# Local attention on one core: the first head group's products with V move behind the next slot's projections, and the transposed probabilities get one PSUM bank

## The reference, cut to what matters

```
qkv = shift_tokens(x) @ Wqkv            # 128 -> 3 * 1024
q, k = l2norm(q) * qs, l2norm(k) * ks   # 16 heads of 64
q, k = rotary(q), rotary(k)
sim  = q @ k.T * 8, windows of 32 tokens, each sees itself and the one before
out  = softmax(sim) @ v @ Wo ; x1 = x + out
xn   = layernorm(shift_tokens(x1))
x2   = x1 + (xn @ W1a + b) * gelu(xn @ W1g + b) @ W2 + b2
```

## Time and profile before

| what | value |
|---|---|
| time, median of 3 runs | 2543.07 us (2542.53 to 2543.28) |
| profiled execution | 2539.95 us, span of its instructions 2538.1 us |
| PE busy | 2370.2 us, 93% of the span |
| DVE, ACT, POOL busy | 77%, 68%, 61% |
| mean granted TensorE clock | 0.985 of full speed |

### The profile page before, as it was taken

One profiled execution on the slowest core, in us unless ns is written; L12 is line 12 of the kernel. 1 busy time (PEld: TensorE's weight loads), 2 busy tenths in 40 slices (PEclk: granted clock), 3 DMA queues, 4 the chain that ended last, 5 costly groups with the idle time before them and its releaser, 6 DMA issues.

```text
span 2538.1 us, 63009 instructions
## 1 busy us (share of the span) xinstructions
PE 2370.2 (93%) x22929; PEld 1578.0 (62%) x22929; DVE 1958.3 (77%) x2967; ACT 1720.5 (68%) x3296; POOL 1552.6 (61%) x1359
## 2 busy tenths in 40 slices
PE   6888789997899999999999999999999999999995
PEld 3555456665466666666666666666666666666664
DVE  4899857776777777777778787777777787787774
ACT  5888545443577777777776776777777777767763
POOL 4777723232666667667666666666676676666662
PEclk8999989999999999999999999999999999999997
DMA  2312110000122122222221221221222222212211
GB/s 73 110 60 64 54 45 1 1 1 9 39 69 62 50 66 69 51 63 61 62 62 51 73 62 50 73 63 50 63 70 53 62 59 65 62 51 73 62 50 48
DMA packets 102906, 140.33 MB, mean 55 GB/s; under 512 B 63040, under 2 KB 63936, under 8 KB 102336
## 3 DMA queue, kind: packets, MB, share of 16 engines
q1 hardware_dynamic: 102848, 139.57, 20.6%
HBM read 56.39 MB, written 1.31 MB: 23 GB/s over the span
## 4 chain that ended last, share of the span: by engine, by line
PE 52%; DVE 16%; issue 5%; ACT 1%; DVEq 1%; DMA 0%; POOL 0%; SPq 0%; POOLq 0%; ACTq 0%
PE f_psA L1751 14%; PE f_psO L1735 9%; PE f_psA L1745 7%; PE f_psD L1755 5%; DVE f_mx L1535 5%; PE f_psS L1715 4%; DVE f_Pr L1542 4%; DVE f_den L1546 3%; PE f_psO L1818 3%; PE f_psS L1697 3%; PE f_psD L1845 3%; PE f_psP L1715 2%; DVE f_x L1592 1%; PE f_psS L1687 1%; DVE f_hT L1558 1%
## 5 line engine op out<-in xcount | busy, mean ns | idle before, releaser
L1751 PE MATMUL f_psA<-f_W,f_xT 128*128 (+1 forms) x1152 | 603.2, 617 | 8.6 <-DVE f_m L1569 5.5
L1344 POOL TENSOR_TENSOR f_Pr<-f_Pr,f_rden 128x384 f32<-128x384 f32 x384 | 310.6, 829 | 484.9 <-DVE f_rden L1548 484.9
L1569 DVE TENSOR_TENSOR f_m<-f_psA,f_tab 128x1024 f32<-128x1024 f32 x384 | 458.8, 1222 | 161.5 <-ACT f_sq L1439 159.0
L1369 POOL TENSOR_TENSOR f_qkr<-f_qkr,f_rn 128x1024 f32<-128x1024 f32 x192 | 360.7, 1897 | 0.1
L1439 ACT ACTIVATE f_sq<-f_psA 128x512 f32<-128x512 f32 x384 | 228.9, 596 | 166.1 <-PE f_psA L1751 161.2
L1361 POOL TENSOR_TENSOR f_qkr<-f_m 128x512 f32<-128x512 f32 x192 | 245.3, 1278 | 142.8 <-DVE f_m L1569 142.8
L1751 PEld LDWEIGHTS f_psA<-f_W,f_xT 128*128 128x128 f32 x1152 | 184.3, 190 | 147.5 <-DVE f_m L1569 70.5
L1735 PE MATMUL f_psO<-f_PT,f_V 96*64 96x64 f32 x6144 | 261.5, 228 | 4.3 <-ACT f_PT L1414 0.2
L1735 PEld LDWEIGHTS f_psO<-f_PT,f_V 96*64 96x64 f32 x6144 | 211.1, 138 | 69.1 <-issue 54.7
L1535 DVE TENSOR_REDUCE f_mx<-f_psS 128x8 f32<-128x768 f32 x192 | 178.8, 931 | 89.0 <-PE f_psS L1697 89.0
L1362 POOL TENSOR_TENSOR f_qkr<-f_m 128x512 f32<-128x512 f32 x192 | 243.3, 1267 | 0.0
(11 more groups left out here) (166 smaller groups left out, 4578.4 us busy)
## 6 DMA issues: line engine op xcount, KB each, us to landing
f_V<-f_Vt SPq DMA_DIRECT2D x96, 384.0 KB, 4.2
f_V<-f_Vt SPq DMA_DIRECT2D x96, 256.0 KB, 3.6
f_W<-in_f_W SPq DMA_DIRECT2D x48, 344.0 KB, 3.6
m_Cb<-m_BC_rows SPq DMA_DIRECT2D x64, 256.0 KB, 3.1
f_W<-in_f_W SPq DMA_DIRECT2D x48, 296.5 KB, 4.2
f_V<-f_Vt SPq DMA_DIRECT2D x48, 128.0 KB, 5.4
f_xsA<-xall SPq DMA_DIRECT2D x97, 32.0 KB
f_xsA<-xall SPq DMA_DIRECT2D x97, 31.8 KB
```

What stands on the lines that cost most here:

```text
L1344: pool.tensor_tensor(pv, pv, rv.unsqueeze(3).broadcast_to([P, 2, 2, KEYS]), ALU.mult).then_inc(Pr_ready[g][j], 1)
L1369: pool.tensor_tensor(qv, qv, rn[:, j * H:(j + 1) * H].unsqueeze(2).broadcast_to([P, H, DH]), ALU.mult).then_inc(qkr_ready[j], 1)
L1569: dve.tensor_tensor(m12[:, j, :, half].rearrange("p m (h d) -> p m h d", d=DH), psA[n % 2][:, :].rearrange("p (h d) -> p h d", d=DH).unsqu ...
L1751: pe.matmul(psA[n % 2][:, :], xT[:, t, :], weights(i, W_QKV + n * 512, 512), start=True, stop=True).then_inc(A_full[n_fill], 1)
```

## The change

Unit v's group 0 is now split. Only its first four heads are transposed at the end of the slot (`transpose_probs(0, 0, v)`). The other transposes and all of its products with V run in the next slot, between `project(1)` and the transposes of q and k, mixed with the remaining projections and the group-1 transposes. All four transposes of a unit use the one bank psP, so each waits for ACT's copy of the one before, and psS holds nothing but scores. The token transpose and `scores(1)` change places with `project(4)`; in the E slot the `w1(0, 0)` and `w1(0, 1)` come ahead of the projections; in the D slot the gate products of chunks 0 and 1 come later. On POOL, `rotate` of k stands between the last two `normalise_probs`, and `scale` of k opens the next slot. On DVE, `gated` moves ahead of `maximum(v, 0)`, and x2 comes ahead of hatC. The ACT order follows. The same matrix products and element-wise operations are done.

```diff
@@ GpSimd, slot @@
-                if "A" in stages:
-                    rotate(u, t, 1)
-                if "B" in stages:
-                    normalise_probs(v, 0, 0)
-                    normalise_probs(v, 0, 1)
+                if "B" in stages:
+                    scale(v, q, 1)
                 if "A" in stages:
                     scaled_tables(u + 1, i + t, 1 - t)
                     rotate(u, t, 0)
                 if "B" in stages:
-                    normalise_probs(v, 1, 0)
-                    normalise_probs(v, 1, 1)
-                if "A" in stages:
-                    scale(u, t, 0)
-                    scale(u, t, 1)
+                    normalise_probs(v, 0, 0)
...
+                if "B" in stages:
+                    normalise_probs(v, 0, 1)
+                if "A" in stages:
+                    scale(u, t, 0)
+                if "B" in stages:
+                    normalise_probs(v, 1, 0)
+                if "A" in stages:
+                    rotate(u, t, 1)
+                if "B" in stages:
+                    normalise_probs(v, 1, 1)
@@ VectorE, slot @@
+                if "E" in stages:
+                    dve.wait_ge(ge_ready, (i - 1) * 3)
+                    gated(2)
+                if "A" in stages:
                     table_products(2)
                     table_products(3)
...
+                if "E" in stages:
+                    dve.wait_ge(ge_ready, (i - 1) * 3)
+                    gated(0)
+                    gated(1)
                 if "B" in stages:
                     maximum(v, 0)
                     less_maximum(v, 0)
...
-                if "C" in stages:
-                    dve.wait_ge(rstdC_ready, wu + 1)
-
-                    at_least(dve, xn_full, i - 1)
-                    dve.tensor_scalar(hatC[:, t, :], xsC[:, t, :], momC[:, 0:1], rstdC[:, :], ALU.subtract, ALU.mult).then_inc(hatC_ready, 1)
                 if "E" in stages:
                     dve.wait_ge(w2_full, i - 1)
                     dve.wait_ge(x1b_ready, (i - 1) * 2)
                     alone(dve, passed)
                     dve.tensor_tensor(tiles_of(i - 2), psD[0][:, T2:2 * T2].rearrange("p (t d) -> p t d", d=D), tiles_of(i - 2), ALU.add).then_inc(x2_done, 2)
+                if "C" in stages:
+                    dve.wait_ge(rstdC_ready, wu + 1)
+
+                    at_least(dve, xn_full, i - 1)
+                    dve.tensor_scalar(hatC[:, t, :], xsC[:, t, :], momC[:, 0:1], rstdC[:, :], ALU.subtract, ALU.mult).then_inc(hatC_ready, 1)
@@ TensorE @@
-                def transpose_probs(g, j):
-                    unit = (v, wu)[g]
+                def transpose_probs(g, j, unit):
 
                     pe.wait_ge(Pr_ready[g][j], unit + 1)
-                    if g != j:
-
-                        pe.wait_ge(S_free[1], unit + 1)
+                    if j == 1:
+                        pe.wait_ge(P_free[g][0], unit + 1)
                     elif g == 1:
-                        pe.wait_ge(P_free[0][0], unit + 1)
-                    elif "C" in stages:
-                        pe.wait_ge(P_free[1][1], wu + 1)
-                    dst = probs_bank(g, j)
+                        pe.wait_ge(P_free[0][1], unit + 1)
+                    else:
+                        at_least(pe, P_free[1][1], unit)
...
                 if "B" in stages:
-                    transpose_probs(0, 0)
-                    transpose_probs(0, 1)
-                    times_v(0, 0)
-                    times_v(0, 1)
+                    transpose_probs(0, 0, v)
```

More of the change, by code:

```diff
@@ L1227, in at_least @@
                 eng.wait_ge(s, n)
-        def probs_bank(g, j):
-            return psP if g == j else psS[:, g, :].rearrange("p (n q) -> p n q", q=P)
         def bias_col(n):
@@ L1408, in slot, with evacuate_probs @@
                 u, v, wu = i * 2 + t, i * 2 + (t - 1), i * 2 + (t - 2)
-                def evacuate_probs(g, j):
-                    unit = (v, wu)[g]
+                def evacuate_probs(g, j, unit):
                     act.wait_ge(P_full[g][j], unit + 1)
-                    act.activation(PT[:, j, :, :], probs_bank(g, j)[0:KEYS, :, :], ACT.Copy).then_inc(P_free[g][j], 1)
+                    act.activation(PT[:, j, :, :], psP[0:KEYS, :, :], ACT.Copy).then_inc(P_free[g][j], 1)
                 def evacuate_v(j):
@@ L1454, in gate_gelu @@
                     act.activation(ge[0:FC[c], c, :], src[0:FC[c], :], ACT.Gelu, bias=bias_col(3 + c)[0:FC[c], :]).then_inc(ge_ready, 1)
+                if "A" in stages:
+                    square(0)
+                if "B" in stages and q == 1:
+                    act.activation(kT[:, 1, :, 0:WIN], kT[:, 0, :, P:P + WIN], ACT.Copy).then_inc(kprev_ready, 1)
+                if "A" in stages:
+                    square(1)
+                if "C" in stages:
+                    evacuate_probs(0, 1, wu)
                 if "D" in stages:
                     act.preload_act_table_set(GELU)
-                if "A" in stages:
-                    square(0)
-                if "D" in stages:
                     act.wait_ge(xn_full, i - 1)
@@ L1465, in slot @@
                 if "A" in stages:
-                    square(1)
-                if "B" in stages and q == 1:
-                    act.activation(kT[:, 1, :, 0:WIN], kT[:, 0, :, P:P + WIN], ACT.Copy).then_inc(kprev_ready, 1)
+                    square(2)
+                if "C" in stages:
+                    evacuate_probs(1, 0, wu)
+                if "A" in stages:
+                    square(3)
+                if "C" in stages:
+                    evacuate_out(0, wu, t)
                 if "D" in stages:
@@ L1602, in slot @@
                     dve.tensor_scalar(rn[:, H:2 * H], rn0[:, H:2 * H], 1e12, None, ALU.min).then_inc(rn_ready, 1)
-                if "E" in stages:
-                    dve.wait_ge(ge_ready, (i - 1) * 3)
-                    gated(0)
-                    gated(1)
                 if "C" in stages:
@@ L1757, in w1 @@
                         ins.then_inc(full[bank_of(c)[1]], 1)
+                if "E" in stages:
+                    pe.wait_ge(ge_ready, (i - 2) * 3 + 2)
+                    w1(0, 0, a_full)
+                    w1(0, 1, a_full)
                 if "A" in stages:
@@ L1762, in slot @@
                     project(0)
+                    project(1)
+                if "C" in stages:
+                    transpose_probs(0, 1, wu)
                 if "D" in stages:
@@ L1771, in slot @@
                     ins.then_inc(xn_full, 1)
-                if "A" in stages:
-                    project(1)
+                if "C" in stages:
+                    times_v(0, 0, wu, t)
                 if "E" in stages:
-                    pe.wait_ge(ge_ready, (i - 2) * 3 + 2)
-                    w1(0, 0, a_full)
-                    w1(0, 1, a_full)
                     pe.wait_ge(ge_ready, (i - 1) * 3)
                     w1(0, 2, a_full)
+                if "A" in stages:
+                    project(2)
+                if "C" in stages:
+                    transpose_probs(1, 0, wu)
+                if "A" in stages:
+                    project(3)
+                if "D" in stages:
+                    pe.wait_ge(w1_loaded, (i - 1) * 16)
+                    pe.wait_ge(xnT_ready, i - 1)
+                    w1(1, 2, gate_full)
+                if "C" in stages:
+                    times_v(0, 1, wu, t)
                 if "D" in stages:
@@ L1819, in slot @@
                     ins.then_inc(wo_full, 1)
-                if "B" in stages:
-                    scores(1)
                 if "A" in stages:
-                    project(4)
                     if "D" in stages:
@@ L1829, in slot @@
                     transpose_tokens(u + 1, i + t, 1 - t)
+                if "B" in stages:
+                    scores(1)
+                if "A" in stages:
+                    project(4)
                     project(5)
                 if "B" in stages:
-                    transpose_probs(0, 0)
-                    transpose_probs(0, 1)
-                    times_v(0, 0)
-                    times_v(0, 1)
+                    transpose_probs(0, 0, v)
                 if "E" in stages:
```

62 lines of the change are left out of this document (20 added, 42 removed).

## The result

| | before | after |
|---|---|---|
| median, range | 2542.80 us (2541.84 to 2543.28, 4 runs) | 2501.38 us (2500.28 to 2502.40, 4 runs) |
| profiled execution, span | 2539.95, 2538.1 us | 2502.4, 2500.6 us |
| ratio after / before | | 0.9837, 95% interval 0.982 to 0.9855 |

The changed kernel is 1.6% faster: 41 us by the medians, 37.5 us by the two profiled spans. 2509 us had been forecast.

What follows compares the result with a forecast made beforehand. It took a cycle of PE and DVE waiting for one another as the bound. 0.77 us won less 0.04 lost, times 46 iterations, is 34 us off 2543: 2509 us, range 2450 to 2552.

Steps and rivals of the forecast that it cites:

- its own case: Whole kernel: the forecast of 2509 us, with a middle part of 2485 to 2525 us; chance 0.57.
- The rival of PE's own list: Loop: DVE comes earlier than counted, so only PE's sum is left; 95 us won, 2448 us; chance 0.13.
- The slower rival: E to D: hatC waits behind POOL's k rotation, 2.5 us on the path; 2624 us, or 2567 with one half; chance 0.14.
- a late POOL: POOL's chain starts 0.8 us later than counted, k transposes are late by 0.6 us; no gain, 2543 us; chance 0.16.
- What PE does at the slot's end: Behind W (start of the instruction after the output projection): E slot starts at +3.46 us, D slot at +4.90.
- D to E: From W in the D slot to W in the E slot: 17.76 us against 18.53, 0.77 us won.
- E to D: From W in the E slot to W in the D slot: 20.18 us against 20.14, nothing won, with hatC held by POOL.
- Not held, it is 0.4 us sooner: E to D: without POOL's hold on hatC, `project(2)` starts 0.4 us sooner; the total would be 18 us less.
- end about where it did: DVE behind W: L1601 will find POOL in a normalisation and end at about the same time as before.
- What would show it: Signs: period near 37.9 us, short waits of `project(2)` for the first table product, E slot's hatC near 0.7 us.
- The one bank costs nothing: Transposes through psP: PE work of 0.67 us or more lies between ACT's copies, so no cost unless ACT is late.
- I put 0 for all eight: Slots outside the loop: gain and lose alike, 0 in all; last slot's four transposes in series cost 1 to 2 us.

Runs made afterwards that it cites:

- e1: Changed kernel with the layer norm's statistics taken of x1 itself, not its token-shifted copy; hatC still reads the shifted copy: 2450.33 us, ratio 0.9639.
- e5: Changed kernel with the second residual x2 put back behind hatC in DVE's list: 2501.21 us, ratio 0.9837.
- e8: Changed kernel with DVE's group-1 denominators ahead of the layer norm's statistics: 2612.54 us, ratio 1.0289.
- e7: Changed kernel with transposed probabilities going to psP and psS as before, the new order kept: 2502.83 us, ratio 0.9841.
- e3: Kernel before with only one part of the change, all four transposes going to psP: 2673.46 us, ratio 1.052.
- e12: Changed kernel, D slot's tile only: group-1 denominators ahead of statistics; root and hatC in the E slot, hatC behind the second table product: 2490.68 us, ratio 0.9797.
- e9: Changed kernel, both slots: group-1 denominators ahead of statistics; root and hatC moved into the next slot, hatC's transposes later: 2516.30 us, ratio 0.9898.

## Why the prediction was right

It forecast 2509 us, with 2485 to 2525 as its own case; 2501.38 is in that, and the period of 37.83 us is the "near 37.9" that it named. The rival of PE's own list is out: e1 gains 51 us with PE's list as it was. The slower rival did not come, since hatC got in ahead of the rotation, nor did a late POOL: `scale` of q ran from +4.31 to +6.2, as counted.

- **What PE does at the slot's end** was right: the E slot starts at +3.55 (forecast +3.46), the D slot at +4.92 (+4.90).
- **D to E**, 0.77 us won, measured 0.75. Two errors of one size cancel in it: `project(2)` starts at +7.95, not +8.1, and from there to the next W it is 9.83 us, not 9.66. The 0.17 us more of the second part are small pieces: 0.09 for the two projections, which now stand apart (0.96 and 0.95 us, not 1.82 for both), and at least 0.07 where the k transposes wait for POOL, whose scaling of k ends at 1518.90:

```profile
1516.99 1.91 POOL L1365 TENSOR_TENSOR f_qkr<-f_qkr,f_rn 128x1024 f32<-128x1024 f32 x1
1518.27 0.69 PE L1728 MATMUL f_psO<-f_PT,f_V 96*64 96x64 f32 x16
1518.95 0.66 PE L1738 MATMUL f_psA<-ident,f_qkr 128*128 128x128 f32 x4
```

The products with V of 1518.27 take 0.68 us to the next start, where the others take 0.61 or 0.62. So POOL ended at +12.56 (forecast +12.5), and the slack, put at 0.2 us, was none.
- **E to D**, 0.04 us lost, measured 0.09 won. hatC was held, as chosen. The mis-sized term is when it ends: I put it at +7.8, 0.3 us behind POOL's instruction (+7.5). POOL's instruction ended at +7.59, and hatC at +7.67, 0.08 us behind it. So hatC took 0.47 us and not the 0.7 named as the sign. The table products started at +7.59, and `project(2)` at +8.94, not +9.15; from there to the next W it was 11.11 us, against 11.03.
- **"Not held, it is 0.4 us sooner"** and the 18 us that I hung on it were wrong. e5 frees hatC and gets 0.07 us: x2 and an issue gap take its place in DVE's list. The hold itself is there: in every row here a `tensor_scalar` that came second ended behind the POOL instruction that was there first, and the hatC of e5, there at 1529.52 before POOL at 1529.68, took 0.31 us. The Trainium skill, "SBUF — State Buffer", section "Who interferes with whom", says of a VectorE instruction in a 2-port mode and a GpSimd instruction that whoever issues first has the shared ports for the whole instruction and the other blocks; the traces agree with that for DVE as the second. For POOL as the second they don't show it: its instruction of 1529.68 took the usual 0.83 us, though hatC ran on to 1529.83. What the hold costs is another question: freeing hatC in E to D was worth 0.07 us in e5, and the longer holds of e8 delayed `project(2)` by 0.97 and 0.57 us.
- **L1601 will "end about where it did"**: it takes 0.36 us now, not 0.68, ending 0.02 us behind POOL's instruction (1528.14 and 1528.12). That is +4.02, where it had been +4.31, with no effect on the sum, since the statistics wait for the DMA.
- **What would show it**: the short wait of `project(2)` is there in D to E (0.45 us, 39 times). In E to D the wait stands at the transposes of hatC ahead of it (0.57 us), and e5 shows that the table product is behind it all the same.
- **The one bank costs nothing**: right (e7), and it needs the new order (e3).
- **"I put 0 for all eight" slots outside**: the parts are +1.3 us ahead of the loop and -3.0 us behind it. The 1 to 2 us named for the tail were put down to the wrong place: the four transposes through one bank cost nothing there, and the loss is in the last feed-forward part, where the 1.2 GHz level and a wait for ACT were not counted. The sum, -1.7 us, is near 0 by luck.
- **The median**: 0.73 x 46 = 34 us was forecast and 39 us found in the loop, which makes 6 of the 8 us between 2509 and 2501; the slots outside take 2 back. The other 4 come from the profiled executions: that of before lies 2.9 us under its median, and that of after 1.0 us over its own.

The text on the change said that the token transpose and `scores(1)` change places with `project(4)`. Only the token transpose moves, to stand ahead of `scores(1)`; `scores(1)` had stood ahead of `project(4)` already. No term of the sum rests on it.

## What to carry to other kernels

Where two engines drive one another round a loop, take the differences of starts of one instruction in each half of the period, and follow the other engine's chain between them: PE was 98% busy before and after, and still gave up 0.84 us per iteration. Such a change is worth what its weakest place allows, so its parts can't be priced one by one: the bank alone costs 131 us in the old order and nothing in the new, and one POOL instruction's place is worth 31 of the 41 us. When an instruction leaves the path, ask first what stands next in the same engine's list, and which instruction of another engine it will now meet.

## What the runs showed of the hardware

- The hold between a `tensor_scalar` on DVE and a POOL instruction shows as a longer DVE row, with no wait beside it. hatC, 0.31 us when free, took 0.47 (after), 0.61 (e1), 0.82 (e12), 1.10 (e9), 1.23 and 1.28 us (e8). In each of these it ends 0.08 to 0.09 us behind the POOL instruction that was running, and it was never held by more than one of them, though POOL's instructions follow each other without a gap. The longest of these was 1.26 us.
- The table products, `tensor_tensor` on float32 with one input in PSUM, were not stretched: two of them took 2.34 us where they started with POOL's rotation (1531.71 after) and 2.36 in e5. One took 1.22 us before, at 1519.5, where POOL ran nothing.
- The granted clock of the kernel after was 0.78 from 2465 to 2475 us, where PE was busy for 4.14 of 10 us, and 0.50, the 1.2 GHz level, from 2475 to 2500 us. The 12 W2 products there took 2.90 us instead of 1.58.
